# Latent attention: row maxima and exponentials taken over two PSUM banks at a time

## What is computed

```python
# _L1_xattn_ref: 4 sequences of 256 rows, context 1601 x 64, H = 16 heads
q_hk  = (hidden_q @ Wq.T).reshape(B, S, H, K)
q_big = rope(einsum('bshk,hkq->bshq', q_hk, w_kc_q))
kv_r  = rope(kv_c)                                   # 1601 keys
q_r   = einsum('bshq,hqr->bhsr', q_big, W_qr)
k_r   = einsum('bld,hdr->bhlr', kv_r, W_kr)
attn  = softmax(einsum('bhsr,bhlr->bhsl', q_r, k_r), axis=-1)
ctx_c = einsum('bhsl,bld->bhsd', attn, kv_r)
out   = einsum('bhsd,hkd->bhsk', ctx_c, w_kc_kv).reshape(...) @ Wo.T
```

## Time and profile before

| | us |
|---|---|
| median of 3 runs (2053.9 to 2057.25) | 2056.48 |
| the profiled execution | 2054.35 |
| its span | 2053.0 |
| iterations of the latent block in the trace | 861 to 1723 |

### The profile page before, as it was taken

How to read it: one execution, slowest core, us unless ns; L and a number is a source line. 1 busy time by engine, 2 the same in 40 slices (tenths; PEclk the granted TensorE clock), 3 DMA queues, 4 the chain that set the end, 5 groups by cost and what they waited for, 6 DMA issues and landing times.

```text
span 2053.0 us, 42322 instructions
## 1 busy us (share of the span) xinstructions
PE 1820.9 (89%) x15964; PEld 1538.4 (75%) x15964; DVE 1289.8 (63%) x3373; ACT 1084.0 (53%) x2729; POOL 602.3 (29%) x542
## 2 busy tenths in 40 slices
PE   6988978958986999879999999999999996894995
PEld 6888876744655766679999999999999986673663
DVE  5566555651225555468888888888888886774222
ACT  4656653311212433368888888888888872331221
POOL 5533320022222300234434444444444430003221
PEclk9999998968996999999999999999999997995998
DMA  4000008312229000000000000000000003202233
GB/s 154 11 1 1 1 16 339 107 52 58 47 37 267 19 2 2 21 11 11 11 11 11 26 11 11 11 11 11 11 11 1 1 1 144 114 3 76 37 47 64
DMA packets 51862, 91.72 MB, mean 45 GB/s; under 512 B 4592, under 2 KB 43632, under 8 KB 49232
## 3 DMA queue, kind: packets, MB, share of 16 engines
q1 hardware_dynamic: 42784, 77.64, 11.4%
q0 software_dynamic: 8160, 10.29, 3.2%
q10 hardware_dynamic: 720, 1.09, 0.2%
HBM read 56.13 MB, written 32.87 MB: 43 GB/s over the span
## 4 chain that ended last, share of the span: by engine, by line
PE 70%; DVE 18%; issue 4%; POOL 3%; ACT 3%; DMA 2%; SPq 0%; ACTq 0%; DVEq 0%; POOLq 0%
PE bank L99 58%; PE bank L2293 9%; DVE a_t L630 2%; DVE e_st L2446 2%; DVE e_PT_lo L2465 1%; DVE d_nm L1286 1%; PE bank L1590 1%; DVE a_t L627 1%; PE bank L187 1%; POOL c_rows L1874 1%; POOL g_rows L1874 1%; PE bank L434 1%; DVE f_nm L1286 1%; DVE d_nm L1285 1%; PE bank L1569 1%
## 5 line engine op out<-in xcount | busy, mean ns | idle before, releaser
L2446 DVE TENSOR_REDUCE e_st<-bank 128x1 f32<-128x401 f32 x512 | 291.5, 570 | 143.3 <-PE bank L99 135.7
L2383 ACT ACTIVATE e_P<-bank,e_st 128x400 f32<-128x400 f32 (+1 forms) x512 | 307.1, 600 | 104.9 <-DVE e_st L2450 104.1
L2465 DVE TENSOR_TENSOR e_PT_lo<-bank,e_PT_hi 128x512 fp32r<-128x512 f32 (+1 forms) x448 | 287.9, 643 | 0.0
L2293 PE MATMUL bank<-ident,e_P 128*128 128x128 f32 (+1 forms) x1664 | 260.4, 276 | 17.3 <-DVE e_PT_lo L2465 6.8
L2398 ACT CAST e_PT_hi<-bank 128x512 fp32r<-128x512 f32 (+1 forms) x448 | 248.2, 554 | 26.7 <-PE bank L2293 12.2
L99 PE MATMUL bank<-e_PT_hi,e_kv 128*128 128x256 f32 (+1 forms) x832 | 250.6, 321 | 0.0
L2293 PEld LDWEIGHTS bank<-ident,e_P 128*128 128x128 f32 (+1 forms) x1664 | 196.4, 141 | 53.7 <-issue 38.2
L99 PE MATMUL bank<-e_PT_lo,e_kv 128*128 128x256 f32 (+1 forms) x832 | 217.2, 281 | 0.0
L99 PE MATMUL bank<-e_KT,e_qk_hi 128*128 128x402 f32 x512 | 194.9, 381 | 10.0 <-ACT e_P L2383 6.5
L99 PE MATMUL bank<-e_KT,e_qk_lo 128*128 128x402 f32 x512 | 177.4, 346 | 0.0
L99 PEld LDWEIGHTS bank<-e_PT_lo,e_kv 128*128 128x128 f32 (+1 forms) x832 | 159.6, 192 | 0.0
(11 more groups left out here) (449 smaller groups left out, 4950.8 us busy)
## 6 DMA issues: line engine op xcount, KB each, us to landing
c_wall<-in_c_w SPq DMA_DIRECT2D x8, 1536.0 KB, 18.2
g_wall<-in_g_w SPq DMA_DIRECT2D x8, 1536.0 KB, 18.2
c_rows<-normed SPq DMA_DIRECT2D x9, 1040.0 KB, 12.0
g_rows<-normed SPq DMA_DIRECT2D x9, 1040.0 KB, 13.7
e_stage<-in_e_w SPq DMA_DIRECT2D x16, 416.0 KB, 3.3
c_xs<-c_rows SPq DMA_DIRECT2D x23, 130.0 KB, 2.1
g_xs<-g_rows SPq DMA_DIRECT2D x23, 130.0 KB, 2.1
landing<-in_a_wo SPq DMA_DIRECT2D x2, 1024.0 KB, 6.1
```

The source lines that it names most:

```text
L2293: last = pe.transpose(o[0:rows, c * SEQ + i * P:c * SEQ + (i + 1) * P], p[:, i, k0:k0 + rows], ident[:])
L2383: act.activation(Pm[u % 2][:, i, j * PIECE:j * PIECE + n], bank[score_bank[j]][:, 0:n], ACT.Exp, bias=s[:, i, 4:5], accum_out=s[:, i, j:j ...
L2446: last = dve.tensor_reduce(s[:, i, j:j + 1], bank[score_bank[j]][:, 0:PIECE + 1], AX.X, ALU.max)
L2465: dve.tensor_tensor(lo, bank[tb_bank[at % 2]][0:rows, 0:n * SEQ].rearrange("p (c n) -> p c n", c=n), hi.bitcast(F32), ALU.subtract).then_i ...
```

## The change

Pieces are scored in pairs: pieces 0 and 1 in the steps with `j` = 1, pieces 2 and 3 in those with `j` = 2, none in the others. DVE takes one maximum over two banks (802 values) in steps 1, 2, 5 and 6, and a pair's negated maxima are joined by a minimum of one element. ACT takes one exponential over two banks (800 values) in steps 0, 1, 4 and 5; the last key has an exponential of its own with one element, and the row sum adds it from `e_P`. `exped` now counts pairs. `absorb_q` is moved from step 1 to step 0.

```diff
+                SCORED_BESIDE = (), (0, 1), (2, 3), ()
...
                     def score(u, i, j):
-                        s, k, o = 8 * u + 4 * i + j, qk[u % 2], bank[score_bank[j]]
+                        pair, k, o = 4 * u + 2 * i + j // 2, qk[u % 2], bank[score_bank[j]]
...
-                        if s >= 4:
-                            pe.wait_ge(*exped.at(s - 3))
+                        if pair >= 2 and j % 2 == 0:
+                            pe.wait_ge(*exped.at(pair - 1))
...
-                            if half == 0 and u is not None:
-                                score(u, 1, j)
-                            elif half == 1 and after is not None:
-                                score(after, 0, j)
-                            if step == 1 and after is not None:
+                            for piece in SCORED_BESIDE[j]:
+                                if half == 0 and u is not None:
+                                    score(u, 1, piece)
+                                elif half == 1 and after is not None:
+                                    score(after, 0, piece)
+                            if step == 0 and after is not None:
                                 absorb_q(after)
...
+                    def exponentials(u, i, pair):
...
                         act.wait_ge(*maxed.at(2 * u + i + 1))
+                        x, p, at = st[u % 4], Pm[u % 2], 2 * PIECE * pair
+                        last = act.activation(p[:, i, at:at + 2 * PIECE].rearrange("p (a n) -> p a n", a=2),
+                                              psum[:, 2 * pair:2 * pair + 2, 0:PIECE], ACT.Exp, bias=x[:, i, 4:5],
+                                              accum_out=x[:, i, pair:pair + 1])
+                        if pair == 1:
+                            last = act.activation(p[:, i, CTX - 1:CTX], bank[score_bank[3]][:, PIECE:PIECE + 1], ACT.Exp,
+                                                  bias=x[:, i, 4:5])
+                        last.then_inc(*exped.up())
...
-                            if u is not None:
-                                exponential(u, half, j)
+                            if u is not None and j < 2:
+                                exponentials(u, half, j)
...
+                    def maxima(u, i, pair):
+                        x = st[u % 4]
+                        dve.wait_ge(*scored.at(8 * u + 4 * i + 2 * pair + 2))
+                        last = dve.tensor_reduce(x[:, i, 2 + pair:3 + pair], psum[:, 2 * pair:2 * pair + 2, 0:PIECE + 1],
+                                                 AX.XY, ALU.max, negate=True)
+                        if pair == 1:
...
+                            dve.tensor_tensor(x[:, i, 4:5], x[:, i, 2:3], x[:, i, 3:4], ALU.min).then_inc(*maxed.up())
...
-                        dve.tensor_reduce(s[:, i, 5:6], s[:, i, 0:4], AX.X, ALU.add).then_inc(link.sem, 1)
+                        dve.scalar_tensor_tensor(x[:, i, 5:6], x[:, i, 0:1], x[:, i, 1:2], Pm[u % 2][:, i, CTX - 1:CTX],
+                                                 ALU.add, ALU.add).then_inc(link.sem, 1)
...
-                            if half == 0 and u is not None:
-                                maximum(u, 1, j)
-                            elif half == 1 and after is not None:
-                                maximum(after, 0, j)
+                            if j in (1, 2) and half == 0 and u is not None:
+                                maxima(u, 1, j - 1)
+                            elif j in (1, 2) and half == 1 and after is not None:
+                                maxima(after, 0, j - 1)
```

More of the change, by code:

```diff
@@ L2286, in turn @@
                         n, rows = keys_of(g)
-                        pe.wait_ge(*exped.at(8 * u + 8))
+                        pe.wait_ge(*exped.at(4 * u + 4))
                         if at >= 2:
@@ L2376, in upper_qk @@
                         act.copy(qk[m % 2][0][:], bank[aux][:, 0:SEQ]).then_inc(*qk_hi.up())
-                    def exponential(u, i, j):
-                        if i == 0 and j == 0 and u >= 2:
+                    def exponentials(u, i, pair):
+                        if i == 0 and pair == 0 and u >= 2:
                             act.wait_ge(*turned.at(GROUPS * (u - 1)))
                         act.wait_ge(*maxed.at(2 * u + i + 1))
-                        n, s = PIECE + (j == 3), st[u % 4]
-                        act.activation(Pm[u % 2][:, i, j * PIECE:j * PIECE + n], bank[score_bank[j]][:, 0:n], ACT.Exp,
-                                       bias=s[:, i, 4:5], accum_out=s[:, i, j:j + 1]).then_inc(*exped.up())
+                        x, p, at = st[u % 4], Pm[u % 2], 2 * PIECE * pair
[6 more added lines that the diff above has]
+                        last.then_inc(*exped.up())
                     def keep_context(u):
@@ L2441, in lower_qk @@
                                           ALU.subtract).then_inc(*qk_lo.up())
[L2443 to L2447, removed]
+                    def maxima(u, i, pair):
[4 more added lines that the diff above has]
+                        if pair == 1:
                             last.then_inc(link.sem, 1)
                             dve.wait_ge(link.sem, link.step())
-                            dve.tensor_reduce(s[:, i, 4:5], s[:, i, 0:4], AX.X, ALU.max, negate=True).then_inc(*maxed.up())
+                            dve.tensor_tensor(x[:, i, 4:5], x[:, i, 2:3], x[:, i, 3:4], ALU.min).then_inc(*maxed.up())
                     def row_sums(u, i):
-                        s = st[u % 4]
-                        dve.wait_ge(*exped.at(8 * u + 4 * i + 4))
-                        dve.tensor_reduce(s[:, i, 5:6], s[:, i, 0:4], AX.X, ALU.add).then_inc(link.sem, 1)
+                        x = st[u % 4]
+                        dve.wait_ge(*exped.at(4 * u + 2 * i + 2))
+                        dve.scalar_tensor_tensor(x[:, i, 5:6], x[:, i, 0:1], x[:, i, 1:2], Pm[u % 2][:, i, CTX - 1:CTX],
+                                                 ALU.add, ALU.add).then_inc(link.sem, 1)
                         dve.wait_ge(link.sem, link.step())
-                        dve.reciprocal(s[:, i, 6:7], s[:, i, 5:6]).then_inc(link.sem, 1)
+                        dve.reciprocal(x[:, i, 6:7], x[:, i, 5:6]).then_inc(link.sem, 1)
                         link.step()
@@ L2488, in vector @@
                     lower_qk(0)
-                    for j in range(4):
-                        maximum(0, 0, j)
+                    for pair in range(2):
+                        maxima(0, 0, pair)
                     latent.lower_o(0, bank[aux])
```

## The result

| | before | changed |
|---|---|---|
| median, us | 2055.19 (4 runs, 2053.12 to 2057.25) | 2173.73 (4 runs, 2170.0 to 2176.39) |
| ratio, 95% interval | 1 | 1.0571 (1.0559 to 1.0584) |
| span of the profiled execution, us | 2053.0 | 2174.0 |
| mean of four iterations of the latent block, us | 12.90 | 14.69 |

The kernel became slower by 119 us, where 52 us were forecast (2108, range 2078 to 2134). The direction was right; the forecast loss was less than half of what came. All iteration times here are distances between the turns of step 0 in the trace, a mean of four in a row (three with a weight fold, one without), taken around 1250 us.

What follows compares the result with a forecast made beforehand. PE, 98.6% busy in the latent block, was taken as the bound. New waits 0.79 + 0.79 less old 0.71 gave +0.87 us an iteration, times 60 = 52 us; 2054.35 + 52 = 2106, median 2108 us, range 2078 to 2134.

Steps and rivals of the forecast that it cites:

- PE's own work: Latent block: PE's matmul time in a mean iteration without waits, 12.90 - 0.71 = 12.19 us, unchanged by the change.
- The first new wait, turn 3 behind `lower_pt` 1: Step 3: PE waits for `lower_pt` of group 1, which follows the pair's maximum on DVE; 0.79 us an iteration.
- The second, `absorb_q` behind the `add` or POOL's query: Step 0: `absorb_q` waits for DVE's `add` or POOL's query, whichever is later; 0.79 us an iteration.
- The forecast's 1.6: Step 0: one of four forecast starts of `absorb_q` behind turn 0 (1.5, 1.5, 1.6 and 1.8 us).
- The sentence on the access overhead: DVE maxima: with 125 ns PSUM access overhead a merged pair costs 1.02 us, leaving the sum as it is within 2 us.
- the sentence on the small operations: ACT and DVE: single-element exponentials and the minimum, at most 0.16 us, hide; on DVE the minimum takes the old one's place.
- The rival of the falling clock: Latent block: a tenth of it at the 1.2 GHz level, 6 iterations some 12 us longer each, 2180 us; 5%.
- one of the named signs of being wrong, a clock below 1.00 in the block: Latent block: the prediction called itself wrong if PE's clock leaves 1.00 there.
- The rivals of no loss: Whole kernel: faster, new waits hidden, 2014 us, 6%; about level, 2072 or 2061 us, 9%.
- the faster rival: Latent block: new waits are hidden, so 0.71 x 60 = 43 us go, 2014 us; 6%.

Runs made afterwards that it cites:

- e11: Changed kernel with one-input minimum and row sum, `absorb_q` back in step 1, row sums moved to the ends of steps 3 and 4; 2021.74 us.
- e1: Changed kernel with the minimum and the row sum both turned into one-input reductions; 2115.45 us, ratio 1.0283.
- e9: Kernel before plus an unused one-element sum with two SBUF inputs behind each reciprocal; 2100.02 us, ratio 1.0210.
- e10: Kernel before plus the same unused sum as a one-input reduction behind each reciprocal; 2062.81 us, ratio 1.0025.
- e3: Changed kernel with `lower_pt` put ahead of the pair's maximum on DVE; 2181.48 us, ratio 1.0591.

## Why the prediction was wrong

*PE's own work* (12.19 us) was right: e11 comes to 12.32.

*The first new wait, turn 3 behind `lower_pt` 1* (0.79 us): right, in its place, its cause and its size. 0.76 us in the changed kernel, plus 0.03.

*The second, `absorb_q` behind the `add` or POOL's query* (0.79 us, starts 1.5, 1.5, 1.6 and 1.8 behind turn 0): right for a kernel without held instructions. With one-input forms the four starts are 1.41, 1.41, 1.46 and 1.77, a mean 0.09 below the forecast one. In the changed kernel they are 1.69, 1.82, 1.81 and 2.99. The forecast's 1.6 is given without a working. A small wait ahead of `project_out` (0.10 and 0.20 us in two of four) is left in e1 and was not in the sum, so that e1 meets the forecast partly because small errors cancel. The sentence on the access overhead is a little off as well: 1.02 in place of 0.99 adds up to 0.03 us to each term, so up to 4 us and not 2.

*The step that failed* is the sentence on the small operations: "the one-element minimum (at most the 0.16 of the four-value maximum) hide there too; on DVE the minimum takes the old one's place". I bounded a new form by the row of an old one that does the same arithmetic on the same tile, and overlooked that it reads two SBUF operands where the old one read one, while POOL, which I had just timed for the query, was busy at that very place. The minimum took up to 0.88 us. The row sum, for which I gave no bound, up to 0.68. In the latent block the kernel before could not show a hold, since DVE's instructions there with two tensor operands take one of them from PSUM. But its trace has the sign elsewhere, in the first attention block, where I did not look. One line of DVE, twice with the same shape and two operands in SBUF, first alone and then beside a POOL operation:

```profile
6.99 0.69 DVE L609 TENSOR_TENSOR a_wkv_lo<-landing,a_wkv_hi 128x512 fp32r<-128x512 f32 x1 [0.21 <-ACT a_wkv_hi L502]
...
16.68 1.28 POOL L725 TENSOR_TENSOR a_kT_lo<-a_t,a_kT_hi 128x512 fp32r<-128x512 f32 x1 [0.73 <-ACT a_kT_hi L516]
16.86 1.65 DVE L609 TENSOR_TENSOR a_wkv_lo<-landing,a_wkv_hi 128x512 fp32r<-128x512 f32 x1
```

It takes 1.65 us instead of 0.69 and ends 0.55 behind POOL's end, so it seems to do most of its work only then. This pair, read ahead of the change, would have put the question.

The Trainium skill states it (SBUF — State Buffer, Who interferes with whom): a DVE instruction with two SBUF inputs contends with a GpSimd instruction that reads SBUF, and one with at most one does not, outside the modes that use two ports. The traces agree on both: 62 of 62 minima, 62 of 62 row sums and 61 of 61 sums in e9 are held, none of 61 in e10. The prediction did not weigh this rule at all.

*How 52 forecast became 119.* e1 is 2115 us against 2108 forecast. The rest is the 59 us between e1 and the changed kernel. In the iterations it is 14.69 - 13.79 = 0.90 us, some 54 us. The profiled executions differ by 62 us (spans 2174.0 and 2112.4), and about 7 us of that come from the clock. The longest iterations, with 2.1 us of wait ahead of `absorb_q`, drop to the lower level in seven places between 992 and 1648. One of them, in the columns of the earlier trace rows:

```profile
1050.40:1053.70 3.30, 3.30 (x15) 3.29 (x15) 0.98 (x3) 2.29 (x7) 0.00 (x0) 0.50 0.00 0
```

The granted clock is 0.50, the 1.2 GHz level, behind an idle stretch of 1.92 us and with the matmuls of `absorb_q` at 0.21 instead of 0.12 us. Such an iteration takes 16.7 to 17.5 instead of 16.0, together 7 us. The same idle stretch stands in the iterations of 16.0, at the higher level (1228.69 above), so the runs do not show what decides. Neither the kernel before nor e1 has such a stretch between 900 and 1690. The rival of the falling clock was thus true in a tenth of the size that I gave it, and one of the named signs of being wrong, a clock below 1.00 in the block, did appear.

*The rivals of no loss* are out in the form in which they were put. But the change's idea was sound: pairs of banks, with the row sums and the minimum in one-input forms, `absorb_q` left where it was and the row sums moved into DVE's idle time, beat the kernel before by 34 us (e11), of the 43 that the faster rival named.

## What to carry to other kernels

When a small instruction replaces another, compare where its operands come from, not only its size: on DVE beside a busy POOL, a second SBUF operand turned 0.16 us into the rest of POOL's instruction. Look for such a form in the whole trace, not only in the block that is changed. Merging work into fewer, larger instructions removes cover as well as overhead, so each instruction that stands behind the merged one needs its deadline checked, and a step that is moved takes its cover from the next wait. Before turning the order round, look at who feeds the instruction that is put first; in e3 it was ACT, whose own row was behind.

## What the runs showed of the hardware

- A DVE instruction of one element with two SBUF tensor operands, started while a POOL `tensor_tensor` ran, ended with that instruction every time (0.61 us on average for the minimum, 0.80 in e9, 0.14 to 0.21 otherwise). One of 512 elements took 1.65 us instead of 0.69 and ended 0.55 behind POOL's. The one-element form with a pointer scalar was not held (0.21 us always), and `lower_pt`, with one operand in PSUM and one in SBUF, was not either (183 of 448 began beside a POOL operation, 0.69 us at most).
- A maximum over two PSUM banks in one operand costs per value what one bank does: 0.987 us for 802 values against 0.570 for 401, so 1.04 ns each, the same as from 4 values (0.16) to 401, and no price for the second bank.
- An exponential over two banks with its accumulator takes 0.93 us, where two single ones take 1.20 (each with 0.2 more to read the accumulator).
